# A cross-attention and mixture-of-experts kernel: the first norm folded into the query weights and the exponential's scale, and the projections of all but the first group of tiles placed inside the attention steps

## The chip, the core and the metric

The kernel runs on one core of a Trainium2 chip. A core has five engines that work side by side and meet only through semaphores: TensorE (matmuls, PE in the profile), VectorE (DVE), ScalarE (ACT), GpSimd (POOL) and SyncE (SP), which here issues most transfers. Each engine takes its instructions in order. TensorE reads SBUF and writes PSUM, which the kernel divides into eight banks of 512 fp32 columns. The metric is the device time of one execution in microseconds; for the kernel before it is 194.75 us, the median of three runs.

## What is computed

The reference is one transformer layer on x of 32 batches, 64 rows and 128 columns, with a second input ctx of the same shape and a mask over ctx's rows. Cut to what matters:

```python
x = x + xattn(layernorm(x), ctx, ctx, mask, Wq, Wk, Wv, Wo)   # 16 heads of 8
x = x + moe(layernorm(x), router, 16 experts of 64, top 2, a shared expert)

# layernorm: (x - mean) / sqrt(var + 1e-5), no weights
# xattn: scores = einsum(q, k) / (8 ** -0.5); masked scores = -1e9; softmax; @ v; @ Wo.T
```

The kernel does not write -1e9 into scores. It replaces each masked key by the mean of its batch's valid keys, so that such a key never holds the row's maximum alone, and it gives masked keys no share in the values and in the denominator. That mean is what "keys' mean" means below.

## The kernel before

The 2048 rows are 16 tiles of 128 rows (two batches each), in four groups of four tiles (GT = 4, GROUPS = 4). All tensors stay in SBUF. The work has three parts.

**Projection, by group.** VectorE takes the moments of x (norm1: four bn_stats, four bn_aggr), GpSimd makes 1/sqrt(var + eps) (rstd1_of: an addition and a power), VectorE scales x (scale1). TensorE's project(g) makes the values from ctx transposed, transposes the scaled x, multiplies the masked ctx by a mixing matrix (identity plus mean, built on ScalarE and GpSimd by mask_row_of and mix_of), and then makes queries (wq) and keys (wk), eight passes each. ScalarE copies what TensorE makes out of PSUM: the transposed x, the mixed ctx, then queries and keys into q_all and k_all. VectorE writes the values, times a share, into v_all.

**Attention, by tile, as a pipeline.** step(t) on each engine works on several tiles at once: scores of tile t + 1, transposes and values of tile t, the output projection of tile t - 1, the second norm and the router of tile t - 2. On TensorE its order is scores(0), values_as_rows, transposes(0), scores(1), attention_transposed, transposes(1), norm_transposed, output_projection, values(0) and (1), router. GpSimd builds the block-diagonal operands q_blk and k_blk of tile t + 2 (q_block, k_blocks). VectorE subtracts the row maximum from the scores, ScalarE takes the exponential with the constant scale SCORE_SCALE. peel(step, LEAD), with LEAD = -1, runs the step ahead of tile 0; before, it stands between the projection of group 2 and that of group 3. Steps 0 to 15 follow the last projection. ScalarE's step t begins with casting one sixteenth of the experts' weights (w_hi).

**Experts, by group.** 36 units of gate, up and down products, each as three products of split operands.

Order is set by hand: each engine's program is a list, and semaphores order the engines. The SP queue loads x of group 0, the constants, then ctx transposed, ctx and x by groups, the second half of ctx into buffers that are used again, then all expert weights at once. ScalarE's queue loads the two masks, the attention weights and the router's bias.

In the rows, bank is a PSUM tensor, L964 the scores, L945 the transposes of the probabilities, L954 the values of a step, L903 queries and keys, L879 the values of a group, L649 the scaling of x, L784 values into v_all, L426 and L418 the two block operands.

Of the kernel before, what the change touches and what calls it, by code (L numbers as in the profile page):

```python
# [15 lines left out]
P = 128  # L16
# [20 lines left out]
W_STEP = W_MOE // TILES  # L37
SCORE_SCALE = float(DK) ** 0.5


def build_program(nc, x, ctx_nat, ctx_t, mask_row, mask_col, w_att, router_bias, w_moe, consts, out):
    stack = ExitStack()
    with stack:
# [26 lines left out]
        mix_all = sb("mix_all", [P, TILES, P])  # L70
# [15 lines left out]
        xn = [sb(f"xn{p}", [P, GT, D]) for p in range(2)]  # L86
        ctx_sb = [sb(f"ctx_sb{p}", [P, GT, D]) for p in range(2)]
        ctxv_sb = [sb(f"ctxv_sb{p}", [P, GT, D]) for p in range(2)]
        ctxt_sb = [sb(f"ctxt_sb{p}", [P, GN]) for p in range(2)]
        xt_sb = [sb(f"xt_sb{p}", [P, GN]) for p in range(2)]  # L90
        cmix_sb = [sb(f"cmix_sb{p}", [P, GN]) for p in range(2)]
        stats1 = [sb(f"stats1_{p}", [P, GT, 6]) for p in range(2)]
        mv1 = [sb(f"mv1_{p}", [P, GT, 2]) for p in range(2)]
        rstd1 = [sb(f"rstd1_{p}", [P, GT]) for p in range(2)]
        veps1 = [sb(f"veps1_{p}", [P, GT]) for p in range(2)]
# [16 lines left out]
        neg_mean2 = [sb(f"neg_mean2_{p}", [P, 1]) for p in range(2)]  # L112
# [17 lines left out]
        hid = [sb(f"hid{k}", [P, GN]) for k in range(2)] + [cmix_sb[1]]  # L130
        hid_hi = [sb(f"hid_hi{k}", [P, GN], F32R) for k in range(3)]
        hid_lo = [sb(f"hid_lo{k}", [P, GN], F32R) for k in range(3)]
        moe_t = cmix_sb[0]
        spread = [mix_all[:, k * GT:(k + 1) * GT, :].rearrange("p t k -> p (t k)") for k in range(SPREADS)]
# [5 lines left out]
        s_x = [sem(f"s_xload{g}") for g in range(GROUPS)]  # L140
        s_const = sem("s_const")
        s_mask_col = sem("s_mask_col")
        s_mask_row = sem("s_mask_row")
        s_wproj = sem("s_wproj")
        s_wmoe = sem("s_wmoe")
        s_ctx = [sem(f"s_ctx{p}") for p in range(2)]
        s_ctxt = [sem(f"s_ctxt{p}") for p in range(2)]
# [5 lines left out]
        s_vcol = sem("s_vcol")  # L153
        s_ctxv = sem("s_ctxv")
        s_mrow = sem("s_mrow")
        s_mean = sem("s_mean")
        s_mix = sem("s_mix")
# [9 lines left out]
        s_xn = sem("s_xn")  # L167
        s_xt = sem("s_xt")
        s_xt_sb = sem("s_xt_sb")
        s_cmix = sem("s_cmix")  # L170
        s_cmix_sb = sem("s_cmix_sb")
# [27 lines left out]
        s_nmean2 = sem("s_nmean2")  # L199
# [40 lines left out]
        xt_ps, cmix_ps, v_ps, q_ps, k_ps = banks[0:5]  # L240
# [6 lines left out]
        at_ps, wo_ps, tail_ps = (bank[:, 0:P] for bank in banks[2:5])  # L247
# [3 lines left out]
        ct_ps = [banks[2][:, (2 + h) * P:(3 + h) * P] for h in range(2)]  # L251
# [84 lines left out]
        def _(sp):  # L336
            sp.dma_start(x_sb[:, 0:GT, :], x_view[:, 0:GT, :]).then_inc(s_x[0], 16)
            sp.dma_start(consts_sb[:, :], consts).then_inc(s_const, 16)
            for p in range(2):
                sp.dma_start(ctxt_sb[p][:, :], ctx_t[:, p * GN:(p + 1) * GN]).then_inc(s_ctxt[p], 16)  # L340
                sp.dma_start(ctx_sb[p][:, :, :], ctx_view[:, p * GT:(p + 1) * GT, :]).then_inc(s_ctx[p], 16)
                sp.dma_start(x_sb[:, (p + 1) * GT:(p + 2) * GT, :], x_view[:, (p + 1) * GT:(p + 2) * GT, :]).then_inc(s_x[p + 1], 16)
            sp.dma_start(x_sb[:, 3 * GT:, :], x_view[:, 3 * GT:, :]).then_inc(s_x[3], 16)
            for p in range(2):
                g = p + 2
                sp.wait_ge(s_ctxv, g - 1)
                sp.dma_start(ctx_sb[p][:, :, :], ctx_view[:, g * GT:(g + 1) * GT, :]).then_inc(s_ctx[p], 16)
                sp.wait_ge(s_v, g - 1)
# [36 lines left out]
        def _(pool):  # L385
# [49 lines left out]
            for g in range(GROUPS):  # L435
# [6 lines left out]
                if g + 1 < GROUPS:  # L442
                    rstd1_of(g + 1)
# [702 lines left out]
```

## Time and profile before

| | us |
|---|---|
| median of three runs (193.85 to 194.76) | 194.75 |
| the profiled execution | 194.68 |
| its span | 192.9 |

| engine | busy us | share of the span | instructions |
|---|---|---|---|
| TensorE | 179.3 | 93% | 1351 |
| VectorE | 168.8 | 87% | 515 |
| ScalarE | 124.6 | 65% | 280 |
| GpSimd | 92.1 | 48% | 148 |

The share of busy time is a mean over parts with different limits. The page's second part cuts the span into 40 slices of 4.8 us: TensorE is at 7, 5, 9, 9, 5 tenths in the first five and at 9 in nearly all others, and its granted clock falls below full speed in slices that lie among the first six. Transfers fill the first six slices and come again, at a third of that share, with the experts. The chain that ended last gives 61% of the span to TensorE, 19% to VectorE and 5% to ScalarE.

### The profile page before, as it was taken

Reading aid. Unit: us, or ns where it says so; the run is one execution under the profiler, and the core shown is the slowest. Engines: PE = TensorE matmul, PEld = TensorE weight load, DVE = VectorE, ACT = ScalarE, POOL = GpSimd, SP = SyncE. Lnnn points to the kernel's source line nnn. Section 1 sums busy time; section 2 is a strip of 40 time slices with the busy share of each in tenths; the row PEclk is TensorE's granted clock in tenths of the full one; section 3 lists DMA queues with packets and bytes.
Section 4 is the critical chain, followed back from the end, with each engine's and each line's share of the span. In section 5 each row is a group of like instructions: output and inputs, shape, how many; then the busy total and the mean of one; then the engine's idle time right before and its main releaser. Section 6 shows DMA issues by size and latency. Waiting matters only on the chain.

```text
span 192.9 us, 4173 instructions
## 1 busy us (share of the span) xinstructions
PE 179.3 (93%) x1351; PEld 131.8 (68%) x1351; DVE 168.8 (87%) x515; ACT 124.6 (65%) x280; POOL 92.1 (48%) x148
## 2 busy tenths in 40 slices
PE   7599599999999999999998799999999999999962
PEld 7497467566666666666666466778888888888841
DVE  6899999589999999989995799988899889988981
ACT  2168374777888888888885855466655665565641
POOL 5746992758988988888786690300000000000000
PEclk9969979999999999999999999999999999999997
DMA  5984910000000000000000174332363236324401
GB/s 135 286 249 92 352 40 0 5 0 0 3 2 5 0 3 0 3 0 2 5 0 3 57 198 139 110 110 82 128 180 115 72 126 171 120 82 126 120 0 54
DMA packets 13202, 15.33 MB, mean 79 GB/s; under 512 B 1665, under 2 KB 8193, under 8 KB 13057
## 3 DMA queue, kind: packets, MB, share of 16 engines
q1 hardware_dynamic: 12608, 14.57, 24.8%
q10 hardware_dynamic: 576, 0.55, 1.2%
q8 instruction: 9, 0.15, 0.3%
q14 instruction: 9, 0.07, 0.1%
HBM read 13.93 MB, written 1.18 MB: 78 GB/s over the span
## 4 chain that ended last, share of the span: by engine, by line
PE 61%; DVE 19%; ACT 5%; issue 5%; POOL 0%; DVEq 0%; POOLq 0%
PE bank L1013 26%; PE bank L964 12%; PE bank L945 5%; PE bank L954 5%; DVE hid L823 2%; PE bank L903 2%; ACT hid_hi L598 2%; PE bank L934 2%; DVE prob L759 2%; PE bank L924 2%; DVE smax L738 2%; DVE xn L649 2%; DVE hid_lo L815 2%; DVE cmix_sb L823 2%; PE bank L893 1%
## 5 line engine op out<-in xcount | busy, mean ns | idle before, releaser
L589 ACT ACTIVATE sig<-bank 128x512 f32<-128x512 f32 x36 | 21.5, 600 | 21.0 <-PE bank L1013 20.4
L964 PE MATMUL bank<-k_blk,q_blk 128*128 128x512 f32 x64 | 34.0, 615 | 0.0
L426 POOL TENSOR_TENSOR k_blk<-k_all,consts_sb 128x512 f32<-128x512 f32 x32 | 32.7, 1045 | 0.0
L1013 PE MATMUL bank<-xt_hi,w_hi 128*128 (+1 forms) x72 | 29.1, 405 | 0.0
L1013 PE MATMUL bank<-xt_lo,w_hi 128*128 (+1 forms) x72 | 28.4, 394 | 0.0
L1013 PE MATMUL bank<-xt_hi,w_lo 128*128 (+1 forms) x72 | 28.3, 393 | 0.0
L542 ACT COPY prob_t<-bank 128x512 f32<-128x512 f32 x32 | 18.8, 586 | 11.5 <-PE bank L945 11.5
L806 DVE TENSOR_TENSOR hid_u<-sig,bank 128x512 f32<-128x512 f32 x32 | 21.9, 684 | 4.2 <-PE bank L1013 2.5
L738 DVE TENSOR_REDUCE smax<-bank 128x8 f32<-128x512 f32 x32 | 21.9, 686 | 2.6 <-PE bank L964 2.6
L759 DVE TENSOR_TENSOR prob<-bank,smax 128x512 f32<-128x512 f32 x32 | 22.0, 687 | 0.6
L547 ACT ACTIVATE prob<-prob 128x512 f32<-128x512 f32 x32 | 20.8, 653 | 0.0
L945 PE MATMUL bank<-consts_sb,prob 128*128 128x128 f32 x128 | 19.2, 273 | 0.0
L598 ACT CAST hid_hi<-hid 128x512 fp32r<-128x512 f32 x24 | 14.9, 621 | 6.4 <-DVE hid L823 6.4
L815 DVE TENSOR_TENSOR hid_lo<-hid,hid_hi 128x512 fp32r<-128x512 f32 x24 | 16.7, 697 | 1.7 <-ACT hid_hi L598 1.0
L1013 PE MATMUL bank<-hid_hi,w_hi 128*128 128x512 f32 (+1 forms) x37 | 15.1, 409 | 2.2 <-DVE hid_lo L815 2.2
L945 PEld LDWEIGHTS bank<-consts_sb,prob 128*128 128x128 f32 x128 | 15.1, 141 | 1.1 <-issue 1.1
L1013 PEld LDWEIGHTS bank<-xt_hi,w_lo 128*128 128x128 f32 x72 | 13.5, 188 | 3.0
L1013 PEld LDWEIGHTS bank<-xt_hi,w_hi 128*128 128x128 f32 x72 | 13.6, 189 | 2.8
L1013 PEld LDWEIGHTS bank<-xt_lo,w_hi 128*128 128x128 f32 x72 | 13.6, 188 | 2.7
L1013 PE MATMUL bank<-hid_hi,w_lo 128*128 128x512 f32 (+1 forms) x37 | 14.4, 390 | 0.0
L1013 PE MATMUL bank<-hid_lo,w_hi 128*128 128x512 f32 (+1 forms) x37 | 14.4, 388 | 0.0
L823 DVE TENSOR_TENSOR hid<-hid_u,mix_all 128x512 f32<-128x512 f32 x20 | 13.9, 697 | 0.0
(116 smaller groups left out, 378.8 us busy)
## 6 DMA issues: line engine op xcount, KB each, us to landing
mix_all<-w_rows SPq DMA_DIRECT2D x64, 128.0 KB, 2.9
w_moe_sb<-w_moe SPq DMA_DIRECT2D x1, 1728.0 KB, 9.9
x_sb<-x SPq DMA_DIRECT2D x4, 256.0 KB, 7.6
ctxt_sb<-ctx_t SPq DMA_DIRECT2D x4, 256.0 KB, 5.9
ctx_sb<-ctx_nat SPq DMA_DIRECT2D x4, 256.0 KB, 5.1
out<-x_sb SPq DMA_DIRECT2D x3, 256.0 KB, 2.3
w_att_sb<-w_att ACTq DMA_DIRECT2D x1, 264.0 KB, 5.8
mrow<-mask_row ACTq DMA_DIRECT2D x1, 256.0 KB, 4.9
```

What stands on the lines that cost most here:

```text
L426: last = nc.gpsimd.tensor_tensor(k_blk[p][:, g, :, :], k_all[:, bass.ds(t, 1), g, :].broadcast_to([P, HG, S]), hmask_sb.rearrange("p (h o) ...
L542: nc.scalar.copy(prob_t[p][:, h * GT:(h + 1) * GT, :], pt_ps[h][:, :].rearrange("p (j q) -> p j q", q=P)).then_inc(s_pt_sb[h], 1)
L547: nc.scalar.activation(prob[q][:, g * GN:(g + 1) * GN], prob[q][:, g * GN:(g + 1) * GN], ACT.Exp, scale=SCORE_SCALE).then_inc(s_exp[g], 1)
L589: nc.scalar.activation(sig[r][:, :], gate_ps[r][:, :], ACT.Silu).then_inc(s_sig, 1)
L738: nc.vector.tensor_reduce(smax[q][:, g * HG:(g + 1) * HG], score_ps[g][:, :].rearrange("p (h s) -> p h s", s=S), AX_X, ALU.max).then_inc(s ...
L759: nc.vector.tensor_tensor(prob[q][:, g * GN:(g + 1) * GN].rearrange("p (h s) -> p h s", s=S), score_ps[g][:, :].rearrange("p (h s) -> p h ...
L806: nc.vector.tensor_tensor(dst[:, :], sig[r][:, :], up_ps[r][:, :], ALU.mult).then_inc(s_hid_u, 1)
L815: nc.vector.tensor_tensor(hid_lo[k][:, cols], hid[k][:, cols], hid_hi[k][:, cols].bitcast(F32), ALU.subtract).then_inc(s_hid_lo, 1)
L823: nc.vector.tensor_tensor(hid[m % 3][:, :], hid_u[r][:, :], spread[k], ALU.mult).then_inc(s_hid, 1)
L945: last = nc.tensor.transpose(pt_ps[h][:, j * P:(j + 1) * P], prob[p][:, c:c + P], ident_sb)
L964: nc.tensor.matmul(score_ps[g][:, :], q_blk[q][:, g, :, :].rearrange("p b s -> p (b s)"), k_blk[q][:, g, :, :].rearrange("p h s -> p (h s) ...
L1013: last = nc.tensor.matmul(out, w, moving, start=start and k == 0, stop=stop and k == 2)
```

## The change

For queries, the mean of x is taken out by a centring matrix that is multiplied into the query weights (wqc = (I - 1/128) wq, times SCORE_SCALE), and 1/sqrt(var + eps) of each row is applied later, as the scale of the exponential. x arrives transposed as a further input, so there is no scaling and no transposing of x for the queries. The moments of x are still taken, with one column of statistics per tile. Masked keys: TensorE makes each batch's mean of ctx as two columns per tile (key_means), and VectorE copies it with a predicate over the masked columns of ctx transposed (mean_keys), after the values have been made from it. The mixing matrices, the masked ctx and their copies go.

Only group 0 is projected ahead of the attention. Values and means of group 1 come there too; queries and keys of group 1 stand in step -1, group 2 in step 0, group 3 in steps 1 and 2. GpSimd makes rstd1_of(0) ahead of the first blocks. Nearly all buffers of inputs hold all groups, so that no load waits. Expert weights come in four loads; the cast of w_hi moves to the end of ScalarE's step. The bias of the second norm is one GpSimd instruction from mean and rstd, without VectorE's neg_mean. at_ps and wo_ps share a bank now, and other banks move.

The core of the diff, in its order:

```diff
@@ sync: loads
+            def load_group(g):
+                cols, tiles = slice(g * GN, (g + 1) * GN), slice(g * GT, (g + 1) * GT)
+                sp.dma_start(ctxt_all[:, cols], ctx_t[:, cols]).then_inc(s_ctxt[g], 16)
+                sp.dma_start(ctx_all[:, tiles, :], ctx_view[:, tiles, :]).then_inc(s_ctx[g], 16)
+                sp.dma_start(xt_all[:, cols], x_t[:, cols]).then_inc(s_xt[g], 16)
...
             sp.dma_start(consts_sb[:, :], consts).then_inc(s_const, 16)
...
+            load_group(0)
+            load_group(1)
+            load_x(0)
+            load_group(2)
+            load_experts(0)
+            load_x(1)
+            load_group(3)
...
@@ gpsimd
+            pool.wait_ge(s_const, 16)
+            pool.wait_ge(s_half, 3)
             rstd1_of(0)
...
+            for t in range(2):
+                pool.wait_ge(s_q_sb, 1)
+                q_block(t, t, first=True)
+                pool.wait_ge(s_k_sb, 1)
+                k_blocks(t, t)
...
             def step(t, p, on):
...
+                if t == 1:
+                    rstd1_of(1)
+                if t in (3, 4):
+                    rstd1_of(t - 1)
...
@@ scalar
             act.dma_start(mcol8[:, :], mask_col).then_inc(s_mask_col, 16)
-            act.dma_start(mrow8[:, :], mask_row.broadcast_to([P, TOKENS])).then_inc(s_mask_row, 16)
             act.dma_start(w_att_sb[:, :], w_att).then_inc(s_wproj, 16)
...
+            act.wait_ge(s_wqc, 1)
+            nc.scalar.mul(wqc_sb[:, :], wqc_ps, SCORE_SCALE).then_inc(s_wqc_sb, 1)
...
             def step(t, p, on):
                 q = 1 - p
                 if isinstance(t, int) and t == TILES - 4:
                     tanh_of(0)
-                if on(0):
-                    cols = bass.ds(t * W_STEP, W_STEP)
-                    nc.scalar.copy(w_hi[:, cols], w_moe_sb[:, cols]).then_inc(s_w_hi, 1)
...
                 def exponentials(g):
                     act.wait_ge(s_sub[g], t + 2)
+                    if (t + 1) % GT == 0:
+                        act.wait_ge(s_rstd1, (t + 1) // GT + 1)
                     nc.scalar.activation(prob[q][:, g * GN:(g + 1) * GN], prob[q][:, g * GN:(g + 1) * GN], ACT.Exp,
-                                         scale=SCORE_SCALE).then_inc(s_exp[g], 1)
+                                         scale=rstd1[:, t + 1:t + 2]).then_inc(s_exp[g], 1)
...
                 if on(0):
                     transposed(1)
+                if t == 2:
+                    queries(3)
...
+                if t == LEAD:
+                    queries(1)
                 if on(-1):
                     exponentials(0)
...
                 if on(-1):
                     exponentials(1)
-                if isinstance(t, int) and t == TILES - 1:
+                if t == LEAD:
+                    keys(1)
+                if t == 0:
+                    queries(2)
+                    keys(2)
+                if t == 2:
+                    keys(3)
+                if on(0):
+                    if t % (TILES // W_LOADS) == 0:
+                        act.wait_ge(s_wmoe[t // (TILES // W_LOADS)], 16)
+                    cols = bass.ds(t * W_STEP, W_STEP)
+                    nc.scalar.copy(w_hi[:, cols], w_moe_sb[:, cols]).then_inc(s_w_hi, 1)
+                if t == TILES - 1:
                     weights_to_sbuf(0)
...
@@ vector
+            def mean_keys(g):
+
+                dve.wait_ge(s_mask_row[min(g, 1)], 16)
+                dve.wait_ge(s_cm, g + 1)
+                dve.wait_ge(s_v, g + 1)
+                cols = slice(g * GN, (g + 1) * GN)
+                nc.vector.copy_predicated(
+                    ctxt_all[:, cols].rearrange("p (c s) -> p c s", s=S), mrow8[:, cols].rearrange("p (c s) -> p c s", s=S),
+                    cm_ps[g][:, 0:GT * BPT].rearrange("p (c o) -> p c o", o=1).broadcast_to([P, GT * BPT, S]))\
+                    .then_inc(s_pred, 1)
...
+            dve.wait_ge(s_const, 16)
+            nc.vector.tensor_scalar(center_sb[:, :], ident_sb, 1.0 / D, None, ALU.subtract).then_inc(s_center, 1)
...
             dve.wait_ge(s_share, 1)
...
+            denominators(slice(0, GT))
+            mean_keys(0)
+            values_to_sbuf(0)
+            moments(0)
+            mean_keys(1)
+            values_to_sbuf(1)
...
                             ALU.subtract).then_inc(s_sub[g], 1)
+                if t == 0:
+                    mean_keys(2)
+                    values_to_sbuf(2)
+                    moments(1)
+                if t == 1:
+                    mean_keys(3)
+                    values_to_sbuf(3)
+                if t == 2:
+                    denominators(slice(GT, TILES))
+                    moments(2)
+                if t == 3:
+                    moments(3)
...
@@ tensor
             pe.wait_ge(s_half, 1)
             keep_busy(9)
+            for i in range(2):
+                nc.tensor.matmul(pvt_ps[:, i * P:(i + 1) * P], half_sb[:, :], half_sb[:, :], start=True, stop=True)
...
+            keep_busy(3)
+            pe.wait_ge(s_center, 1)
+            pe.wait_ge(s_wproj, 16)
+            nc.tensor.matmul(wqc_ps, center_sb[:, :], wq_sb, start=True, stop=True).then_inc(s_wqc, 1)
+            keep_busy(3)
+            key_means(0)
+            pe.wait_ge(s_wqc_sb, 1)
+            values_of(0)
+            queries(0)
+            keys(0)
+            key_means(1)
+            values_of(1)
...
+                if t == 0:
+                    key_means(2)
+                    values_of(2)
                 if on(-1):
                     pe.wait_ge(s_blk, t + 2)
                     scores(0)
...
                 if on(0):
                     transposes(0)
+                if t == LEAD:
+                    queries(1)
+                if t == 1:
+                    key_means(3)
+                if t == 2:
+                    queries(3)
                 if on(-1):
                     scores(1)
...
                 if on(0):
                     transposes(1)
+                if t == LEAD:
+                    keys(1)
+                if t == 1:
+                    values_of(3)
+                if t == 2:
+                    pe.wait_ge(s_v_sb, GROUPS)
...
                 if on(0):
                     if t == 0:
+                        queries(2)
                         pe.wait_ge(s_vden, 2)
+                    if t == 2:
+                        keys(3)
...
                     values(0)
                     values(1).then_inc(s_pvt, 1)
                 if on(2):
                     router(t - 2, p)
...
+                if t == 0:
+                    keys(2)
```

queries(g) on TensorE waits for x transposed and, from group 2 on, for mean_keys(g); keys(g) waits for mean_keys(g) and for the copy of the keys before (keys(3): of queries(3)); values_of(g) waits for values_to_sbuf(g - 1), that of group 3 for the copy of keys(2); key_means(g) waits for w_mean (group 0), the first predicated copy (group 1), or the copy of the queries before.

## Rows read from the trace of the kernel before

**Rows 1.** windows: length, busy us per engine (instructions), granted clock, DMA share, GB/s
```profile
0.00:27.76 27.76, 22.51 (x139) 18.62 (x139) 24.89 (x69) 14.07 (x32) 19.40 (x28) 0.88 0.67 201
...
27.76:59.92 32.16, 31.85 (x344) 21.05 (x343) 28.14 (x94) 23.90 (x59) 23.58 (x37) 1.00 0.01 2
...
59.92:86.70 26.78, 26.78 (x313) 18.05 (x314) 25.09 (x120) 22.46 (x62) 23.87 (x44) 1.00 0.01 2
```

**Rows 2.** the chain of waits: start us, length us, engine and line
```profile
19.14 3.61 DVE xn L649 x4
...
27.83 1.91 PE bank L964 x4
...
29.74 0.89 PE bank L879 x8
...
31.96 1.88 PE bank L903 x16
...
34.89 0.44 PE bank L945 x4
...
35.33 0.86 PE bank L964 x2
...
37.75 1.05 PE bank L964 x2
...
41.27 0.71 PE bank L954 x32
...
41.98 1.06 PE bank L964 x2
...
59.92 0.95 PE bank L964 x2
```

**Rows 3.** timeline of the front: start us, length us, engine, instruction, idle before
```profile
4.82 0.69 SPq L342 DMA_DIRECT2D x_sb<-x  x1
...
6.46 0.19 DVE L669 TENSOR_TENSOR inv_half<-inv_valid,consts_sb 128x32 f32<-128x32 f32 x1
...
9.58 1.28 ACT L508 ACTIVATE ctxv_sb<-ctx_sb,valid_col 128x128 f32<-128x128 f32 x4 [2.84 <-DMA ctx_sb<-ctx_nat]
...
10.27 0.87 DVE L637 BATCH_NORM_STATS2 stats<-x_sb 128x6 f32<-128x128 f32 x4
...
11.48 1.70 DVE L784 TENSOR_TENSOR v_all<-bank,share_key 64x256 f32<-64x256 f32 x4
```

**Rows 4.** DMA issues of 4.5 to 5 us: SP's eighth transfer, us to landing
```profile
x_sb<-x SPq DMA_DIRECT2D x1, 256.0 KB, 7.6
```

**Rows 5.** groups by line: count, busy us, mean ns, idle before
```profile
L759 DVE TENSOR_TENSOR prob<-bank,smax 128x512 f32<-128x512 f32 x32 | 22.0, 687 | 0.6
...
L399 POOL TENSOR_TENSOR rstd<-veps,neg_half 128x4 f32<-128x4 f32 x4 | 4.1, 1025 | 0.3
...
L418 POOL TENSOR_TENSOR q_blk<-q_all,consts_sb 128x256 f32<-128x256 f32 x16 | 9.9, 616 | 5.0 <-ACT k_all L528 4.5 <-PE bank L964 0.5
...
L426 POOL TENSOR_TENSOR k_blk<-k_all,consts_sb 128x512 f32<-128x512 f32 x32 | 32.7, 1045 | 0.0
...
L538 ACT CAST w_hi<-w_moe_sb 128x216 fp32r<-128x216 f32 x16 | 6.2, 387 | 0.0
```

**Rows 6.** windows: TensorE's idle stretches and the two at half clock
```profile
7.15:9.30 2.15, 0.00 (x0) 0.00 (x0) 2.15 (x3) 0.00 (x0) 2.07 (x2) 1.00 0.96 290
...
9.50:12.90 3.40, 3.40 (x17) 3.40 (x17) 3.25 (x14) 2.05 (x6) 1.18 (x2) 0.50 0.90 274
...
20.70:22.80 2.10, 0.02 (x2) 0.01 (x1) 2.10 (x4) 0.00 (x0) 2.10 (x4) 1.00 0.97 398
...
23.15:26.55 3.40, 3.40 (x17) 2.64 (x17) 3.26 (x12) 2.30 (x6) 2.89 (x5) 0.50 0.41 162
...
102.40:103.40 1.00, 0.20 (x2) 0.03 (x1) 0.89 (x9) 0.10 (x1) 0.76 (x2) 1.00 0.00 0
```

**Rows 7.** timeline, VectorE: the slowest product of two SBUF tiles
```profile
114.11 1.50 DVE L823 TENSOR_TENSOR cmix_sb<-hid_u,mix_all 128x512 f32<-128x512 f32 x1
```

More of the change, by code:

```diff
@@ L84, in build_program @@
         none_valid = sb("none_valid", [P, BATCHES])
[L86 to L95, printed above, removed]
+        center_sb = sb("center_sb", [P, P])
+        wqc_sb = sb("wqc_sb", [P, D])
+        w_mean = sb("w_mean", [P, BATCHES])
+        stats1 = sb("stats1", [P, TILES, 6])
+        mv1 = sb("mv1", [P, TILES, 2])
+        veps1 = sb("veps1", [P, TILES])
+        rstd1 = sb("rstd1", [P, TILES])
         neg_half = sb("neg_half", [P, GT])
@@ L166, in build_program @@
         s_rstd1 = sem("s_rstd1")
[L167 to L171, printed above, removed]
         s_v = sem("s_v")
@@ new lines, in denominators @@
+            def denominators(tiles):
+                for e in range(2):
+                    rows = slice(e * S, (e + 1) * S)
+                    nc.vector.tensor_copy(
+                        v_all[rows, tiles, :, :, e, DK].rearrange("p t b j -> p (t b) j"),
+                        share_key[rows, tiles.start * BPT:tiles.stop * BPT].rearrange("p (c o) -> p c o", o=1)
+                        .broadcast_to([S, (tiles.stop - tiles.start) * BPT, PAIRS])).then_inc(s_vden, 1)
+            nc.vector.memset(v_all[:, 0:GT, :, :, :, :].rearrange("p t b j e d -> p (t b j e d)"), 0.0)\
@@ L862, in keep_busy, with key_means @@
                     nc.tensor.matmul(score_ps[0][:, 0:P], half_sb[:, :], half_sb[:, :], start=True, stop=True)
+            def key_means(g):
+                pe.wait_ge(s_ctx[g], 16)
+                if g == 0:
+                    pe.wait_ge(s_wmean, 1)
+                elif g == 1:
+                    pe.wait_ge(s_pred, 1)
+                else:
+                    pe.wait_ge(s_q_sb, g)
+                for i in range(GT):
+                    t = g * GT + i
+                    last = nc.tensor.matmul(cm_ps[g][:, i * BPT:(i + 1) * BPT], ctx_all[:, t, :],
+                                            w_mean[:, t * BPT:(t + 1) * BPT], start=True, stop=True)
+                last.then_inc(s_cm, 1)
@@ new lines, in values_of, with by_heads @@
+            def values_of(g):
+                pe.wait_ge(s_ctxt[g], 16)
+                if g == GROUPS - 1:
+                    pe.wait_ge(s_k_sb, g)
+                elif g > 0:
+                    pe.wait_ge(s_v_sb, g)
+                for i in range(GT):
+                    c = (g * GT + i) * P
+                    last = nc.tensor.matmul(v_ps[g][:, i * P:(i + 1) * P], ctxt_all[:, c:c + P], wv_sb, start=True, stop=True)
+                last.then_inc(s_v, 1)
+            def by_heads(w, src, g, dst):
+                for hg in range(2):
+                    for b in range(BPT):
+                        last = nc.tensor.matmul(
+                            dst[b * ROWS:(b + 1) * ROWS, hg * GT * S:(hg + 1) * GT * S], w[:, hg * ROWS:(hg + 1) * ROWS],
+                            src[:, g * GN:(g + 1) * GN].rearrange("p (t b s) -> p t b s", b=BPT, s=S)[:, :, b, :],
+                            start=True, stop=True)
+                return last
@@ L1001, in step @@
                     router(t - 2, p)
-                if once and t == TILES - 1:
+                if t == 0:
+                    keys(2)
+                if t == TILES - 1:
                     weights_as_rows(0)
-            for g in range(GROUPS):
-                if g == GROUPS - 1:
-                    peel(step, LEAD)
-                project(g, g % 2, first=g == 0)
+            peel(step, LEAD)
             def three_products(out, w_parts, moving_parts, start, stop):
```

291 lines of the change are left out of this document (104 added, 187 removed).

## The prediction

> **What bounds the kernel now.** Read the table of stretches first [rows 1]. Until 27.76 us, when the first scores run, TensorE is busy for 22.51 of 27.76 us at a mean granted clock of 0.88, and VectorE for 24.89: this is the projection of groups 0 to 2. From 27.76 to 59.92 come the scores of the first tile, the projection of group 3 and steps 0 to 5; from 59.92 on TensorE has no idle time and six steps take 26.78 us, so 4.46 each. The chain of waits [rows 2] says what a step is there: only TensorE's pieces, in a row. Its earlier part holds the VectorE scaling of x (3.61 us for four tiles of group 2), which ends at 22.75 and lets TensorE go on; the first scores stand at 27.83 after three more matmul groups. Step 0 starts at 31.96 + 1.88 = 33.84, step 1 at 37.75, step 2 at 41.98, step 6 at 59.92. What the change does before step 6 decides; after it both kernels issue the same work, but for one place told below. The profiled execution took 194.68 us, 192.9 of them span; the median of the runs is 194.75, so the sum on the one stands for the other.
>
> **The front: when can the first scores run?** Removed from it are the scaling of x, the transposes of x and the mixing matrices for all groups, and groups 1 to 3. What is left for group 0 is a chain over four engines. The SP queue now loads the constants, then three arrays of 256 KB of group 0, three of group 1, and x of group 0 as its eighth. Before, the fourth and eighth had the same bytes ahead of them and landed at 9.58, where ScalarE's wait for it ends [rows 3], and at 4.82 + 7.6 = 12.4 us [rows 3, 4]. Five of the eight lay in rows of 512 bytes, now three do and the others in rows of 2 KB, so I take 11.6 to 12.4 for x. The small VectorE chain on the mask ended with inv_half at 6.65 [rows 3]; the count in it now stands behind two more dummy products on TensorE, and the centring matrix and w_mean come behind it: I take 7.9 for its end, 8.3 for the centring product's copy. With 0.45 for key_means(0), estimated as eight passes of 0.11 like those of the values, 0.89 for values and 0.94 for queries [rows 2], values(0) runs from about 8.6 to 9.6 and the queries to 10.8, where the fourth transfer has landed too. On VectorE, behind values(0), come the predicated copy (0.7, bounded below), the four instructions of values_to_sbuf (1.70) and moments(0), 10.27 to 11.48 before, so 1.21, and a hop [rows 3]. That ends at 9.6 + 0.1 + 0.7 + 1.7 + 1.25 = 13.35 or, if x lands at 12.4, at 13.7. **Here is the wait that the change adds:** on GpSimd rstd1_of(0) stands before the first q_block, so q_block(0), k_blocks(0) and with them TensorE's scores are queued behind moments(0), though queries and keys are there by 12.4. rstd's power is 1.03, with the addition and two hops 1.45; q_block 0.62; two k_blk of 1.05 [rows 5]. The first scores stand at 13.4 + 1.45 + 0.62 + 2.1 + 0.1 = 17.7, against 27.83 to the same measure: 10.1 us earlier.
>
> **What is handed back in the steps.** Group 1 goes into step -1, group 2 into step 0, group 3 into steps 1 and 2. By the chain, scores are 0.88 per half, queries or keys 0.94 (1.88 for both), values 0.89, transposes 0.44 [rows 2]; key_means 0.45 as above.
> - Step -1 up to the scores of tile 1: 0.88 + 0.94 + 0.88 + 0.94, then key_means(2) and values_of(2), 0.45 + 0.89: 5.0.
> - Step 0: scores, transposes, scores are 2.2 (values, below, 0.71) [rows 2]; then queries(2) waits for mean_keys(2), which VectorE does only behind the second row maximum and subtraction. That is 0.15 + 0.6 + 0.7 + 0.75 + 0.1 = 2.3, of which 0.44 hides the other transposes: TensorE stands about 1.9 us. Queued behind are both value halves and keys(2). With 0.94 + 0.71 + 0.94 the step takes 7.1.
> - Step 1: its own 4.23, with key_means(3) and values_of(3) 1.3 more, less 0.2 of waits that they fill: 5.3.
> - Step 2: 4.46 + 1.88, and two waits: 0.3 for att, since values_to_sbuf(3) pushes VectorE back, and 0.9 for keys(3), which needs ScalarE's copy of queries(3), queued behind a probability copy: 7.5.
> - Step 3: 4.5. moments(2), the denominators and moments(3) put 1.25 + 0.7 + 1.25 on VectorE; step 4 pays with a wait of 1.1 for att: 5.6. rstd1_of(2) and (3) put 1.25 each on GpSimd, whose own step is nearly full (23.87 of 26.78 us, [rows 1]); the bias of the second norm comes late in step 5: 5.3.
> Step 6 would start at 17.7 + 5.0 + 7.1 + 5.3 + 7.5 + 4.5 + 5.6 + 5.3 = 58.0, against 59.92: 1.9 us gained of 10.1.
>
> **The clock.** Two stretches in which TensorE was nearly or wholly idle, 2.10 and 2.15 us long, stand right before 3.40 us each at a granted clock of 0.50, which is 1.2 GHz instead of 2.4; an idle time of 0.8 us inside 102.4 to 103.4 is followed by full clock [rows 6]. In the new front TensorE is out of work from about 13.0 (values_of(1)) to 17.7, over 4 us. I expect the half clock when it returns. A whole such stretch costs half of itself, 1.7 us; part may fall into the idle time, and I take 1.3, between 0.8 and 1.7. That leaves 0.6. The Trainium skill ("TensorE: Matmul & The Clock Gate", section "Loop structure matters more than you think") holds that a VectorE copy between matmuls does not break the warm clock and that long DMA waits do. The idle time from 20.7 to 22.8 was a wait for VectorE's scaling, and the half clock came all the same [rows 2, 6]. By that rule the sum would keep its 1.9, and the copies of step 0 would cost nothing beyond their time.
>
> **The rest.** neg_mean goes from VectorE, one instruction on 128x1 in each step: nothing where TensorE bounds the step, and I book nothing. The cast of w_hi moves from the head to the tail of a step. Inside the loop that is the same place in ScalarE's queue; in step 15 it now stands before the copy of the experts' weights, behind which the first silu is queued, and costs its 0.39 there, if nothing covers it [rows 5]; bounds 0 and 0.39, and I book 0.2 lost. The exponential's scale from a column instead of a constant: 0, as the same engine reads such columns in the second norm; bounds -0.1 and +0.1 per tile half, hidden by ScalarE's slack (22.46 of 26.78, [rows 1]). Bank moves of the attention output add no wait I can name: the readers were already ordered. The four loads of expert weights land by about 20 and their first reader is the end of step 0. Extra load of 1 MB (x transposed) lies in a time where the queue runs anyway, behind x of group 0.
>
> No row shows a **predicated copy**. Nearest is the subtraction of a broadcast row maximum, one operand in PSUM and one in SBUF, the same 512 columns: 0.69 [rows 5]. The other end is a product of two SBUF tiles beside a busy GpSimd: 1.50 [rows 7]. I take 0.7. It counts twice on the path (group 0 in the front, group 2 in step 0), so the far end costs 1.6. Less than 0.6 is not to be had from any VectorE row of that width.
>
> Sum: 194.68 - 1.9 + 1.3 + 0.2 = 194.3; with the early steps of the trace some 0.1 longer than the sum of their pieces, **194.4**.
>
> **The rivals.**
> - Faster: the clock stays up, as the page's rule has it, or the half clock falls mostly into the idle time; or x lands 0.8 earlier. 194.68 - 1.9 + 0.2 = 193.0, with the earlier landing 192.2. For it: the idle stretch is so long that some of the low clock must be spent in it. Against it: both restarts in the trace were slow.
> - Slower: a second half-clock stretch, in step 0, at the wait of queries(2) for mean_keys(2). 1.9 us lie between 2.10 (followed by half clock) and 0.8 (not). It decides from there: if the predicated copy is nearer 1.5 the wait is 2.7 and it is likely. Price 1.7: 196.1; with the slow copy 197.7.
> - The change does not do what it says: attention starts early only if its first blocks do. If x landed late, say at 14, the whole lead shrinks by 1.6 and the time is 196.0, by the same GpSimd wait. Rows 3 and 4 speak against it.
>
> **How the numbers follow.** Forecast case (one slow restart, copy 0.7) 0.42, with its own range 193.5 to 195.4; faster rival 0.33 (192.0 to 193.4); slower rivals together 0.25 (195.7 to 197.7). A measurement of this kernel tells about 0.5%, 1 us, from no change. Faster by more: 0.33 and a little of the middle, 0.36; slower by more: 0.27; the rest 0.37. The range leaves out the ends of both rivals: 192.0 to 197.0.
>
> **What would show it.** First scores at 17.7, directly behind GpSimd's k_blk, and moments(0) before that; the clock at 0.50 around 18 to 21; a TensorE wait of about 1.9 us before queries(2) in step 0; scores of tile 1, 2, 3, 4 at about 24, 31, 37, 44; step 6 near 59.3; steps of 4.46 after it. I am wrong if the first scores run before 16, if the predicated copy is over 1 us, if the steps with projections pay less than 8 us together over those of before, or if the steps after step 6 change their length.

## The result and the profile after

The changed kernel takes 199.35 us (median of four runs, 198.24 to 200.11) against 194.3 for the kernel before in the same sittings: ratio 1.026, 95% interval 1.022 to 1.031. It is slower, beyond the range of the forecast (192.0 to 197.0). The profiled execution took 198.24 us, 196.4 of them span, 3.5 more than before. Ratios here leave out executions over 1.5% longer than the fastest of the same kernel, which in experiment 2 takes out the four longest of ten.

First the stretches of the changed kernel, cut at the first scores of each step as [rows 1] was: length, then busy time of PE, PEld, DVE, ACT and POOL with the number of instructions, the granted clock (TensorE's, as a share of full speed), DMA share and GB/s.

```profile
0.00:18.64 18.64, 13.46 (x87) 11.74 (x87) 9.38 (x30) 2.73 (x4) 7.25 (x14) 0.95 0.89 261
18.64:27.03 8.39, 8.39 (x37) 4.15 (x38) 2.77 (x4) 2.40 (x4) 5.13 (x6) 0.70 0.59 208
27.03:34.30 7.27, 5.38 (x63) 3.02 (x61) 5.97 (x16) 2.65 (x5) 2.62 (x3) 1.00 0.00 1
34.30:40.02 5.72, 5.72 (x67) 4.44 (x65) 3.90 (x10) 3.43 (x8) 1.83 (x3) 1.00 0.01 3
40.02:47.62 7.60, 6.89 (x74) 4.02 (x69) 7.30 (x22) 4.57 (x12) 4.06 (x7) 1.00 0.00 0
47.62:63.05 15.43, 14.10 (x159) 9.09 (x158) 14.11 (x70) 12.35 (x32) 13.51 (x24) 1.00 0.01 2
63.05:89.90 26.85, 26.85 (x313) 18.09 (x314) 25.11 (x114) 23.38 (x60) 24.52 (x43) 1.00 0.01 2
...
17.10:18.69 1.59, 0.05 (x1) 0.06 (x1) 0.04 (x1) 0.00 (x0) 1.59 (x3) 0.50 1.13 352
18.69:24.72 6.03, 6.03 (x18) 2.17 (x20) 1.87 (x3) 1.21 (x2) 2.91 (x4) 0.59 0.79 284
```

The first scores stand at 18.64 us instead of 27.76 [rows 1], so 9.1 us are won. Step 6 starts at 63.05 instead of 59.92 [rows 1, 2]: steps -1 to 5 hand back 12.2. (Both are by the chain of waits; in TensorE's timeline the same scores start at 62.96 and 59.77, and the timeline is what the experiments below are cut by.) From step 6 to the end it is 133.35 us against 192.9 - 59.92 = 132.98; the six steady steps are unchanged, 26.85 against 26.78. Step -1, in the second line, is TensorE without idle time but at a mean clock of 0.70; the last two lines show the half clock begin while TensorE is still idle (0.50 from 17.10 on) and end inside step -1: a mean of 0.59 over 18.69 to 24.72 is half clock until about 23.6 and full clock behind it.

Then the timeline of the front (start, length, engine, line, operation, idle time before and what ended it).

```profile
10.82 0.73 DVE L641 COPY_PREDICATED ctxt_all<-mrow,bank 128x512 f32<-128x512 uint8 x1 [2.92 <-PE bank L897]
11.46 1.71 DVE L656 TENSOR_TENSOR v_all<-bank,share_key 64x256 f32<-64x256 f32 x4
13.23 0.87 DVE L629 BATCH_NORM_STATS2 stats<-x_sb 128x6 f32<-128x128 f32 x4
14.14 0.38 DVE L632 BATCH_NORM_AGGREGATE mv<-stats 128x2 f32<-128x6 f32 x4
14.69 0.20 POOL L411 TENSOR_TENSOR veps<-mv,eps_sb 128x4 f32<-128x4 f32 x1 [10.78 <-DVE mv L632]
14.97 1.03 POOL L413 TENSOR_TENSOR rstd<-veps,neg_half 128x4 f32<-128x4 f32 x1
15.97 0.61 POOL L419 TENSOR_TENSOR q_blk<-q_all,consts_sb 128x256 f32<-128x256 f32 x1
16.54 2.04 POOL L427 TENSOR_TENSOR k_blk<-k_all,consts_sb 128x512 f32<-128x512 f32 x2
18.64 2.07 PE L999 MATMUL bank<-k_blk,q_blk 128*128 128x512 f32 x2 [3.96 <-POOL k_blk L427]
```

Read it from below: the scores waited 3.96 us for k_blk, which stood behind q_blk, which stood behind rstd, which waited for the last aggregate of moments(0). The keys of tile 0 had been in SBUF since 13.3 (ScalarE's copy into k_all, 12.74 + 0.59). A piece that only the exponentials need holds back the first matmul of the attention, and with it TensorE.

Last, TensorE's waits in steps 0 to 5, from its own timeline.

```profile
31.67 1.08 PE L903 MATMUL bank<-xt_all,wqc_sb 128*64 128x256 f32 x8 [1.89 <-DVE ctxt_all L641]
...
45.77 1.08 PE L903 MATMUL bank<-ctxt_all,w_att_sb 128*64 128x256 f32 x8 [0.66 <-ACT q_all L501]
...
55.59 0.33 PE L954 MATMUL bank<-consts_sb,att 128*128 128x128 f32 x1 [0.66 <-DVE att L766]
...
61.48 0.33 PE L965 MATMUL bank<-consts_sb,xn 128*128 128x128 f32 x1 [0.67 <-ACT xn L530]
```

queries(2) waits 1.89 us for the predicated copy (step 0), keys(3) 0.66 for ScalarE's copy of queries(3) (step 2), att 0.66 in step 4, the second norm 0.67 in step 5.

### The profile page after: what moved, and what is told of

It is laid out like the page before. It is cut to its first block, busy times and chain, and to the rows that moved or that the text cites. A ratio compares the mean times of both kernels' runs of the same rounds, so it can differ in the third digit from the quotient of the medians.

```text
span 196.4 us, 4094 instructions
## 1 busy us (share of the span) xinstructions
PE 178.6 (91%) x1343; PEld 128.1 (65%) x1343; DVE 159.2 (81%) x491; ACT 116.6 (59%) x253; POOL 84.8 (43%) x140
## 4 chain that ended last, share of the span: by engine, by line
PE 49%; DVE 22%; POOL 8%; DMA 6%; issue 6%; ACT 4%; SPq 3%; DVEq 0%; POOLq 0%
PE bank L1065 25%; PE bank L999 9%; DVE hid L834 4%; DVE smax L755 4%; DMA x_sb<-x 4%; DVE prob L776 3%; PE bank L989 3%; POOL k_blk L427 3%; PE bank L980 3%; PE bank L903 3%; ACT hid_hi L588 2%; POOL rstd L413 2%; DMA spread_all<-w_rows 1%; DVE hid_lo L826 1%; SPq L342 1%
## 5 line engine op out<-in xcount | busy, mean ns | idle before, releaser
L999 PE MATMUL bank<-k_blk,q_blk 128*128 128x512 f32 x64 | 35.8, 643 | 4.0 <-POOL k_blk L427 4.0
L588 ACT CAST hid_hi<-hid 128x512 fp32r<-128x512 f32 (+1 forms) x37 | 22.4, 609 | 12.3 <-DVE hid L834 12.0
L826 DVE TENSOR_TENSOR hid_lo<-hid,hid_hi 128x512 fp32r<-128x512 f32 (+1 forms) x37 | 25.4, 689 | 3.9 <-ACT hid_hi L588 3.5
L523 ACT ACTIVATE prob<-prob,rstd 128x512 f32<-128x512 f32 x32 | 23.8, 743 | 1.8 <-DVE prob L776 1.8
L834 DVE TENSOR_TENSOR hid<-hid_u,spread_all 128x512 f32<-128x512 f32 x32 | 23.0, 719 | 0.1
```

Source lines behind the costliest of these rows:

```text
L523: nc.scalar.activation(prob[q][:, g * GN:(g + 1) * GN], prob[q][:, g * GN:(g + 1) * GN], ACT.Exp, scale=rstd1[:, t + 1:t + 2]).then_inc(s_ ...
L588: nc.scalar.copy(hid_hi[k][:, cols], hid[k][:, cols]).then_inc(s_hid_hi, 1)
L826: nc.vector.tensor_tensor(hid_lo[k][:, cols], hid[k][:, cols], hid_hi[k][:, cols].bitcast(F32), ALU.subtract).then_inc(s_hid_lo, 1)
L834: nc.vector.tensor_tensor(hid[m % 3][:, :], hid_u[r][:, :], spread[k], ALU.mult).then_inc(s_hid, 1)
L999: nc.tensor.matmul(score_ps[g][:, :], q_blk[q][:, g, :, :].rearrange("p b s -> p (b s)"), k_blk[q][:, g, :, :].rearrange("p h s -> p (h s) ...
```

## The experiments

All are edits of the changed kernel unless said otherwise. The rival theory in most of them is that VectorE, ScalarE and GpSimd have no room in steps 0 to 5, so that what is taken away comes back a step later.

**1. The clock alone.** Dummy products (matmuls whose result nobody reads) keep TensorE at work while it waits for GpSimd; nothing else moves.

```diff
             key_means(1)
             values_of(1)
+            keep_busy(13)
```

> Changed kernel with 13 dummy products on TensorE between values_of(1) and the first scores, so that TensorE has work while GpSimd makes rstd1_of(0), q_block(0) and k_blocks(0). Theory A (the half clock after the idle wait is paid on the path): the first scores stay at 18.6 us, the granted clock stays at 1.00 from 14.7 on, step -1 (first scores to those of step 0) falls from 8.39 to 5.6 us, step 0's scores stand at 24.3 instead of 27.0, the time falls by 2.8 us to about 196.5. Theory B (the steps are bound by VectorE's and ScalarE's chains, the clock only fills waits): step -1 gets shorter, but step 0 and step 1 get longer by as much and the time falls by under 0.8 us.

Measured: 196.58 us (196.01 to 197.12), ratio 1.013 [1.009, 1.017].

```profile
14.65:18.69 4.04, 2.44 (x22) 2.25 (x21) 2.25 (x5) 0.00 (x0) 3.86 (x6) 1.00 1.13 322
18.69:24.72 6.03, 6.03 (x36) 3.46 (x37) 2.77 (x4) 2.40 (x4) 5.13 (x6) 1.00 0.81 294
24.72:32.00 7.28, 5.39 (x62) 3.02 (x61) 5.97 (x16) 2.65 (x5) 2.61 (x3) 1.00 0.01 3
```

The first scores stay at 18.69, the clock is 1.00 throughout, step -1 takes 6.03 instead of 8.39, and step 0 is as long as before (7.28 against 7.27). The half clock costs 8.39 - 6.03 = 2.36 us and nearly all of it reaches the end: 2.8 in the medians, 2.2 in the profiled executions. The rival gave under 0.8. The missed number is step -1 itself, 6.03 and not 5.6.

**2. What GpSimd does first.** rstd1_of(0) moves behind the blocks of tile 0.

```diff
-            rstd1_of(0)
             for t in range(2):
...
                 k_blocks(t, t)
+                if t == 0:
+                    rstd1_of(0)
```

> Changed kernel with rstd1_of(0) moved on GpSimd from ahead of the first q_block to behind the k_blocks of tile 0. Theory A (the first scores wait on GpSimd, which waits for moments(0) on VectorE, and the idle time this gives costs the clock too): the first scores stand at 15.5 instead of 18.6, TensorE's idle time before them falls from 4.0 to about 0.9 us, the clock stays at 1.00, step 0's scores stand near 21.1 instead of 27.0, and the time falls by 5 to 6 us, to about 193.8, near or under the kernel before. Theory B (VectorE, busy with values_to_sbuf(1) until 17.2, holds the first row maximum and the exponentials then wait for rstd): the first scores come earlier, but step 0 starts no more than 3 us earlier and the time falls by at most 3.

Measured: 194.71 us, the median of ten (192.24 to 198.06), against 194.64 for the kernel before; ratio 0.993 [0.990, 0.997]. By the median the kernel is level with the one before, by the ratio just below it; against the changed kernel it is 4.6 us shorter, nearer to the 5 to 6 of the first theory than to the at most 3 of the second. Windows of its profiled execution:

```profile
7.75:9.21 1.46, 0.02 (x2) 0.00 (x1) 0.00 (x0) 0.00 (x0) 0.00 (x0) 1.00 0.88 244
11.50:15.00 3.50, 3.50 (x18) 1.76 (x16) 2.82 (x9) 0.83 (x2) 0.61 (x1) 0.52 1.00 261
17.52:23.55 6.03, 6.03 (x37) 3.46 (x38) 4.51 (x9) 2.50 (x4) 5.95 (x8) 1.00 1.07 360
```

Step 0's scores stand at 23.55 instead of 27.03, not at 21.1 as expected. In this execution ctx_all of group 0 landed late; TensorE stood idle for it (first line, 1.46 us) and the half clock came at 11.5 (second line), so queries and keys of group 0 were late and the first scores stand at 17.52. From there on the clock stays up, as expected, and step -1 takes 6.03 (5.6 in the expectation). That the late landing makes up the rest is an inference from this one execution; experiment 5 has the same edit and an earlier landing.

**3. Spreading the moments.** moments(2) and (3) by two tiles a step, rstd1_of(2) and (3) behind steps 5 and 8.

```diff
...
                 if t == 2:
                     denominators(slice(GT, TILES))
-                    moments(2)
-                if t == 3:
-                    moments(3)
+                if t in (3, 4, 6, 7):
+                    stats_of({3: 8, 4: 10, 6: 12, 7: 14}[t])
+                if t in (5, 8):
+                    aggregate(2 if t == 5 else 3)
```

> Changed kernel in which moments(2) and moments(3) are no longer four bn_stats and four bn_aggr in one step (2 and 3), but two bn_stats in each of the steps 3, 4, 6 and 7, and the bn_aggr in steps 5 and 8; rstd1_of(2) and (3) go with them. Theory A (steps 4 and 5 are late because whole groups of moments and rstd stand in one step's queue): the waits of 0.66 (att) and 0.67 (norm) in steps 4 and 5 go, steps 3 to 5 take 14.0 instead of 15.4, time down by about 1.2. Theory B (VectorE has only 0.3 us of room in a step, so the 2.5 us of moments are paid wherever they stand): steps 3 to 8 together take as long as before, time down by under 0.4.

Measured: 198.24 us (198.12 to 199.99), ratio 1.023 [1.017, 1.030], not to be told from the changed kernel. First a window of it, then a line of its GpSimd timeline and one of TensorE's:

```profile
47.77:61.21 13.44, 13.44 (x158) 8.95 (x158) 13.04 (x64) 12.02 (x31) 11.39 (x20) 1.00 0.01 2
```

```profile
61.66 1.03 POOL L413 TENSOR_TENSOR rstd<-veps,neg_half 128x4 f32<-128x4 f32 x1
...
64.99 0.33 PE L977 MATMUL bank<-consts_sb,xn 128*128 128x128 f32 x1 [0.61 <-ACT xn L530]
```

Steps 3 to 5 take 13.44 instead of 15.34 (47.62 to 62.96, both by the timeline), better than the 14.0 expected. But the wait for the second norm turns up in step 6, behind rstd1_of(2), and once more in step 9 behind rstd1_of(3). Steps 3 to 9 together take 32.91 us against 33.20. The rival is right here, though the wait is behind GpSimd, not VectorE: rstd1_of's two instructions, 1.3 us with their hops, are more than a steady step has left (six of them keep GpSimd busy for 24.52 of 26.85 us, the line of 63.05 in the first table), and both are followed by a wait of 0.6.

**4. The wait in step 0.** queries(2) goes behind the values, ahead of keys(2).

```diff
                     if t == 0:
-                        queries(2)
                         pe.wait_ge(s_vden, 2)
...
                 if t == 0:
+                    queries(2)
                     keys(2)
```

> Changed kernel in which TensorE issues queries(2) behind both halves of the values of step 0, ahead of keys(2), instead of ahead of the values. Theory A (TensorE's wait of 1.89 us for mean_keys(2) on VectorE is on the path, and the values have their operands 1.2 us before it ends): 0.6 to 0.7 us of values fill the wait, step 0 takes 6.6 instead of 7.27, the time falls by 0.6. Theory B (step 0 and 1 are bound by VectorE, TensorE's wait is only the sign of it): the wait moves to step 1, no change within 0.3.

Measured: 198.2 us (197.45 to 199.42), ratio 1.023 [1.017, 1.028]. By the medians alone this could be nothing; the trace decides, by step 0 and the wait in it:

```profile
26.74:33.27 6.53, 5.45 (x63) 3.27 (x61) 5.26 (x11) 3.35 (x6) 2.62 (x3) 1.00 0.01 1
```

```profile
31.39 1.08 PE L903 MATMUL bank<-xt_all,wqc_sb 128*64 128x256 f32 x8 [0.77 <-DVE ctxt_all L641]
```

Step 0 takes 6.53 instead of 7.27, the wait 0.77 instead of 1.89, and the profiled execution is 0.79 shorter than the changed kernel's. Of that gain 0.28 was already there ahead of step 0 (8.11 for step -1 against 8.39). But steps 1 to 5 take 28.64 us against 28.66, so what step 0 wins is not handed back in the next steps. So the wait was on the path, as the forecast said.

**5. The order mended.** Experiments 2 and 3 together; the predicated copy of group 2 at the end of step -1, where VectorE is idle, instead of behind step 0's softmax; and in step 15 the copy of the experts' weights ahead of the cast of w_hi.

```diff
...
+                if t == LEAD:
+                    mean_keys(2)
                 if t == 0:
-                    mean_keys(2)
                     values_to_sbuf(2)
...
```

> Changed kernel with four edits of order together: rstd1_of(0) behind the k_blocks of tile 0, mean_keys(2) on VectorE at the end of step -1 instead of the end of step 0, moments(2) and (3) spread over steps 3 to 8, and in step 15 the copy of the experts' weights ahead of the cast of w_hi. Theory A (the loss is made of waits in the queues and of the clock after one of them, not of the folded norm itself): first scores at 15.5 to 17.5, step -1 6.0, step 0 5.4 (its wait of 1.89 gone), steps 1 and 2 5.7 and 7.6, steps 3 to 5 13.5 to 14.1, tail 0.37 less; step 6 near 55 instead of 63.05, the time 190 to 193, under the kernel before. Theory B (VectorE and GpSimd have no room in steps 0 to 5, so a wait taken away appears again in the next step): over half of the gain comes back in steps 1 to 5, the time stays over 194.

Measured: 190.56 us (190.3 to 191.17), ratio 0.984 [0.982, 0.987]: faster than both kernels.

```profile
0.00:15.04 15.04, 12.29 (x86) 10.71 (x87) 7.45 (x26) 2.73 (x4) 6.08 (x12) 1.00 0.85 244
15.04:21.07 6.03, 6.03 (x37) 3.46 (x37) 4.59 (x9) 2.50 (x4) 5.95 (x8) 1.00 1.06 332
21.07:26.38 5.31, 5.31 (x62) 2.93 (x60) 4.81 (x9) 2.65 (x5) 2.96 (x4) 1.00 0.47 178
26.38:32.11 5.73, 5.73 (x68) 4.45 (x66) 5.19 (x16) 3.44 (x8) 1.83 (x3) 1.00 0.01 3
32.11:39.71 7.60, 6.89 (x74) 4.02 (x69) 6.71 (x19) 4.58 (x12) 4.06 (x7) 1.00 0.00 0
39.71:53.15 13.44, 13.44 (x158) 8.96 (x158) 13.05 (x64) 12.01 (x31) 11.37 (x20) 1.00 0.01 2
```

Beside the first table: the front is 3.6 us shorter, step -1 2.36, step 0 1.96, steps 3 to 5 1.90 (by the timeline); step 6 starts at 53.15 instead of 62.96. Steps 1 and 2 are as they were. Behind that, steps 6 to 14 take 1.6 us more than in the changed kernel (53.15 to the scores at 90.76, against 62.96 to 98.96), in steps 6 and 9, which are 0.77 and 0.78 longer, each with a wait of 0.60 for the second norm, as in experiment 3; and from there to the end it is 0.3 more. The gain of 0.37 expected in step 15 isn't to be seen.

**6. The same with dummy products** (8 instead of 3 ahead of key_means(0), 4 behind values_of(1)).

> The kernel with the four edits of order, and dummy products on TensorE in the front: 8 instead of 3 ahead of key_means(0), and 4 behind values_of(1), so that a late landing of the context or the wait for GpSimd leaves TensorE no idle time of over a microsecond. Theory A (what is left of the scatter between executions is the half clock that follows an idle wait for a late load, as in the run with rstd1_of(0) moved, where 1.44 us of idle time for ctx_all stood before 3.5 us at 0.50 to 0.83): the granted clock is 1.00 up to step 6, the times lie within 2 us of each other, median 190 to 191. Theory B (the scatter is in the landings themselves): the times scatter over 3 us or more as without the products, and the median is no lower.

Measured: 191.25 us (190.69 to 191.97), ratio 0.987 [0.984, 0.991]. The clock is 1.00 up to step 6, as expected; but experiment 5 without the products is no slower and scatters no more (0.9 against 1.3 us), so there was no scatter left to explain, and here the first scores stand at 15.87, behind an x_t that landed later. The products buy nothing in this order.

**7. The half clock of the kernel before.** Its two idle waits [rows 6] filled with dummy products.

```diff
-            keep_busy(5)
+            keep_busy(12)
...
+                if g == 2:
+                    keep_busy(7)
                 pe.wait_ge(s_xn, g + 1)
```

> Kernel before, with dummy products in its two idle waits of TensorE: 12 instead of 5 behind the count (7.15 to 9.30 us), and 7 ahead of the transposes of x of group 2 (20.7 to 22.8 us). Theory A (the half clock in a front costs what TensorE has on the path there): both stretches at 0.50 go, but only the second is followed by TensorE work that ends at the first scores, so the first scores stand 1.2 to 1.7 us earlier and the time is 193.0 to 193.5. Theory B (VectorE, busy for 24.89 of 27.76 us, bounds this front and the half clock costs nothing): clock at 1.00, first scores within 0.4 us of 27.76, time unchanged.

Measured: 194.19 us (193.79 to 194.57), ratio 1.000 [0.999, 1.002]. First the two stretches that stood at 0.50 [rows 6], then TensorE's timeline:

```profile
9.50:12.90 3.40, 2.92 (x24) 2.49 (x26) 2.88 (x14) 2.48 (x7) 0.60 (x2) 1.00 0.85 259
23.15:26.55 3.40, 3.40 (x29) 2.38 (x29) 3.26 (x13) 2.73 (x8) 2.96 (x4) 1.00 0.22 86
```

```profile
26.49 1.98 PE L966 MATMUL bank<-k_blk,q_blk 128*128 128x512 f32 x4
...
29.72 0.66 PE L888 MATMUL bank<-consts_sb,xn 128*128 128x128 f32 x4 [0.36 <-DVE xn L649]
...
59.08 1.10 PE L966 MATMUL bank<-k_blk,q_blk 128*128 128x512 f32 x2
```

The clock is 1.00 in both stretches and the first scores stand 1.27 us earlier, as the first theory had it. Then group 3's transposes wait for VectorE's scaling of x, and step 6 is only 0.69 earlier than in the profile of before (59.77 in its timeline). In the median time nothing is left. Part of that is outside the span: the median span is 191.9 us against 192.2 for the kernel before in the same sitting, but the times stand 1.9 to 2.4 us above their spans where those of before stand 1.8, and no trace here shows why. The other executions of the kernel before bear on it without an edit, though what else differs between them is not recorded: five at a mean clock of 1.000 have spans of 191.8 to 192.0, five at 0.973 have 192.5 to 193.0 (the profiled one: 0.976 and 192.9). By these figures I estimate the half clock of before at 0.3 to 0.9 us, where VectorE is busy for most of the front, against the 2.4 in step -1 of the changed kernel. The first theory missed the time (193.0 to 193.5), the second the first scores (within 0.4 us of 27.76).

**8. The waits that were left.** Experiment 5, with keys(3) behind the values of step 2, the denominators of groups 1 to 3 on GpSimd in the front, and moments(2) with rstd1_of(2) in step 2.

```diff
...
                 if t == 2:
-                    denominators(slice(GT, TILES))
+                    moments(2)
...
+                if t == 2:
+                    keys(3)
```

> The kernel with the four edits of order, and three more: keys(3) on TensorE behind the values of step 2 instead of ahead of them; the denominators of groups 1 to 3 on GpSimd in the front, where it is idle until 12 us, instead of on VectorE in step 2; moments(2) whole at the end of step 2 in their place, with rstd1_of(2) at the end of step 2 on GpSimd, which stands 1.4 us idle there, instead of behind step 5. Theory A (the last waits are of the same kind, a late piece in a full queue): the wait of 0.66 for the copy of queries(3) and that of 0.60 for the second norm in step 6 go, the time falls by 1.2 to about 189.4; a wait of 0.6 stays where rstd1_of(3) stands, in step 9. Theory B (VectorE and GpSimd are full from step 2 on): the waits move into steps 3 and 4, and the time stays within 0.4 of 190.6.

Measured: 191.8 us (189.46 to 192.17), ratio 0.985 [0.976, 0.994]. Steps 0 to 6 take 36.38 us (scores at 23.83 and 60.21) against 37.33 in experiment 5 (21.07 and 58.40), so 0.95 of the 1.26 expected; the waits for the copy of queries(3) and for the norm in step 6 are gone, one of 0.31 for xt_hi came in step 2, and the one behind rstd1_of(3) stands in step 9. The front of this execution took back more than that, with the first scores at 16.21 instead of 15.04 and step -1 at 7.62 instead of 6.03:

```profile
15.39:16.21 0.82, 0.00 (x1) 0.00 (x1) 0.79 (x5) 0.00 (x0) 0.82 (x2) 1.00 0.92 324
16.21:19.70 3.49, 3.49 (x10) 1.06 (x10) 3.13 (x7) 0.00 (x0) 3.41 (x5) 0.54 1.08 330
```

ctx_all landed at 9.34 instead of 7.97, and after a wait of 0.82 for k_blk the clock fell.

**9. Experiment 8 with dummy products** (6 ahead of key_means(0), 4 behind values_of(1)).

> The kernel with seven edits of order, with dummy products on TensorE again: 6 instead of 3 ahead of key_means(0), and 4 behind values_of(1). In the profile of the kernel without them an idle wait of 0.82 us ahead of the first scores was followed by 3.5 us at 0.50 to 0.75 of the clock and step -1 took 7.6 us. Theory A (that scatter of 189.5 to 192.2 is the half clock after the idle waits of the front): step -1 6.0 in the profile, the times lie within 1.3 us of each other, median 189.3 to 190.0. Theory B (it is the landing of the loads, ctx_all at 8.0 in one execution and 9.3 in another): the times scatter over 2 us or more and the median is over 190.5.

Measured: 190.74 us (190.15 to 192.07), ratio 0.982 [0.978, 0.985]. Step -1 is back at 6.03, as the first theory had it. But TensorE waited 1.01 us for ctx_all, which landed at 9.10, and the half clock came in the stretch around 12:

```profile
11.00:13.00 2.00, 2.00 (x11) 1.00 (x11) 1.59 (x4) 0.00 (x0) 0.00 (x0) 0.50 1.05 312
```

The scatter stays at 1.9 us and the median is over 190.0, so the first theory's numbers are missed and the second's nearly met (2 us, over 190.5). The landings scatter, and in experiments 2 and 9 the half clock follows a late one. Experiments 5 and 9 can't be told apart.

## Why the prediction was wrong

The forecast's steps against what was measured; the half clock is separated from step -1 by experiment 1.

| term | forecast | measured | difference |
|---|---|---|---|
| first scores at | 17.7 | 18.64 | +0.94 |
| step -1 at full clock | 5.0 | 6.03 | +1.03 |
| half clock in it | 1.3 | 2.36 | +1.06 |
| step 0 | 7.1 | 7.27 | +0.17 |
| step 1 | 5.3 | 5.72 | +0.42 |
| step 2 | 7.5 | 7.60 | +0.10 |
| steps 3 to 5 | 15.4 | 15.43 | +0.03 |
| from step 6 on, against before | +0.2 | +0.37 | +0.17 |

Together 3.92, and 194.28 (the forecast's sum ahead of the 0.1 that it adds at the end) + 3.92 = 198.20 against 198.24 profiled. The waits and their places were right; the steps that failed are sizes, and 3.03 of the 3.92 lie in the first three rows: the price of the half clock (1.3, measured 2.36), step -1 (5.0, measured 6.03) and the chain ahead of the first scores (17.7, measured 18.64), in which the landing of ctx_all had no term. By cause:

- **The size of the half clock.** That it would come was right, and where. Its price was taken from the length of the stretches before, 3.40 us [rows 6], with 1.7 as the upper end. Here 18.69 to 24.72 has a mean of 0.59, so (1 - 0.59)/0.5 of 6.03 us, 4.9, stood at half clock, and that costs 2.4. Part of the low clock did fall into the idle time, as the forecast allowed (17.10 to 18.69 stands at 0.50), but the whole stretch, over 6.5 us, was about twice as long as those before. The length of a stretch in one kernel was taken for a bound in another; no row of before has an idle wait of 4 us.
- **key_means.** Eight passes of 0.11 are 0.88, not the 0.45 that the sum used: an error of arithmetic. The passes measure 0.88 in the front. The sum has 0.43 too little in the front, in step -1 and in step 1, 1.3 in all, and that is all of the miss in step 1.
- **Step -1's other pieces.** At full clock, in experiment 1, scores took 1.06 to the next group's start where the sum had 0.88 (the rows it was taken from run from 0.86 to 1.06), queries and keys 1.01 where it had 0.94, values 0.97 where it had 0.89 [rows 2]: 0.6 over the step.
- **The front.** rstd, q_block and k_block took 0.2 less than the forecast said (14.53 to 18.64 is 4.11, against 4.35 from 13.35 to 17.7). The chain before them was late: ctx_all landed at 8.64 where the sum lets key_means begin at 8.15 (8.6 - 0.45), a term that it does not have, for of the first loads it bounds only the fourth and the eighth. key_means ran to 9.5, and values(0) began at 9.55 instead of 8.6. x, issued at 6.31 where before it was at 4.82, landed at 13.20 instead of at 12.4 at most, in the same moment as VectorE came free (13.17), so its lateness cost next to nothing by itself.

Right were the wait for GpSimd and its place, the predicated copy (0.73 against 0.7), the wait in step 0 (1.89 against 1.9), what the waits of steps 3 to 5 cost together, and the steady steps. Step 2 was partly luck: TensorE is busy for 6.89 us there and idle for 0.71, where the sum had 6.34 and waits of 1.2, and the two errors cancel. The exponential with its scale from a column takes 743 ns against 653 for the constant in before, the upper end of the bound, and is hidden.

**The rivals.** The slower rival named a second half clock in step 0, which did not come: after 1.89 us of idle time the clock is 1.00 in 27.03:34.30. The time came out beyond that rival all the same, by the length of the first stretch, the rest of step -1 and the late front. The faster rival fell with the lines of 17.10 and 18.69: the half clock came, and most of it lay on the path. "x lands late" came in part and was hidden by VectorE.

The rule weighed in the forecast, from the Trainium skill ("TensorE: Matmul & The Clock Gate", section "Loop structure matters more than you think"), says that a VectorE copy between matmuls leaves the clock up and a long DMA wait does not. Step 0 agrees (1.89 us for VectorE's predicated copy, clock 1.00), and so does the 1.46 us wait for a load in experiment 2 (0.52 some 2 us later). The kernel before does not: 2.10 us of idle time for VectorE's scaling stand ahead of 0.50 [rows 6]. The front is outside the rule: what TensorE waited for was GpSimd, and the clock fell.

What stays open: why landings of group 0 differ by over a microsecond from one execution to the next, and what makes up the 0.37 from step 6 on. By TensorE's timeline it is 0.31, of which 0.02 lies ahead of the scores at 98.96 (95.75 in before) and 0.29 behind them, where TensorE waits 0.18 and 1.28 us for the second norm against once 1.15; no experiment tests that. The cast of w_hi was moved back in experiment 5 and no gain can be seen there, so nothing shows the 0.2 that was booked for it.

## What to carry to other kernels

Before work is moved ahead of or behind a pipeline, list for each in-order queue what stands in front of the first instruction that the bounding engine waits for; here a 1.3 us piece on GpSimd, needed only by the first exponentials (at 23.14 us), cost some 3 us of start (18.64 against 15.04 in experiment 5, where ctx_all also landed 0.67 earlier) and 2.4 of clock. An idle wait of the bounding engine is to be priced with the slow stretch that may follow it, and that stretch can outlast the ones seen so far. The same change can be slower or faster than before by order alone: 199.35 as given, 190.56 with four moves.

## What the hardware showed beyond that

The same wait of 0.82 us for k_blk before the first scores was followed by a clock of 0.54 in experiment 8 and of 1.00 in experiment 5; the length of one wait doesn't settle it. (The waits for ctx_all earlier in the two fronts differ, 0.94 and 0.49 us; whether that matters is not shown.) SP's issue of a load is no fixed price: ctx_all of group 1 took 2.26 us to issue in the changed kernel and 0.92 to 1.63 in its eight edits, and the next load is issued only behind it (3.13 + 2.26, then 5.43). GpSimd's power takes 1.03 us on 128x4 and 0.55 on 128x1; from these two sizes one may estimate 0.16 a column beside a fixed 0.39.
